# Reordering the settled slots of a cross-attention and FP4 feed-forward layer, with one ff2 bank for each row half

## The reference, cut to what matters

```python
# x (8, 512, 256); ctx (8, 64, 256); dff 1024; FP4 ffn width 704
y = layernorm0(x)                                    # 1
y = layernorm(y + attention(y, y, y, causal=True)) * g1 + beta1
y = layernorm(y + attention(y, ctx, ctx)) * g2 + beta2      # cross-attention
y = layernorm(y + relu(y @ w1 + b1) @ w2 + b2) * g3 + beta3 # ff1, ff2
x = x + y
xq = fp4(layernorm(x))                               # blocks of 16, scale max/6, round to a grid
h = silu(xq @ fp4(w_gate).T) * (xq @ fp4(w_up).T)
out = x + fp4(h) @ fp4(w_down).T
```

## Time and profile before

| what | us |
|---|---|
| median of 3 runs | 597.99 (596.93 to 598.6) |
| the profiled execution, its own time | 599.96 |
| its span, first to last instruction | 597.4 |
| TensorE busy | 561.2 (94%) |
| VectorE busy | 495.2 (83%) |
| ScalarE, GpSimd busy | 374.4 (63%), 383.1 (64%) |
| mean granted TensorE clock | 0.994 |

### The profile page before, as it was taken

One profiled execution on the slowest core, in us unless ns is written; L12 is line 12 of the kernel. 1 busy time (PEld: TensorE's weight loads), 2 busy tenths in 40 slices (PEclk: granted clock), 3 DMA queues, 4 the chain that ended last, 5 costly groups with the idle time before them and its releaser, 6 DMA issues.

```text
span 597.4 us, 12450 instructions
## 1 busy us (share of the span) xinstructions
PE 561.2 (94%) x4042; PEld 532.7 (89%) x4042; DVE 495.2 (83%) x1222; ACT 374.4 (63%) x778; POOL 383.1 (64%) x463
## 2 busy tenths in 40 slices
PE   4787889999999999999999999999999999999985
PEld 3676789999999999999999999999999999999885
DVE  4989888887988888887988888887978878887776
ACT  3766565766667575766667575766667574756231
POOL 3668657676757667676757667675767656666542
PEclk9999989999999999999999999999999999999989
DMA  7701010010201001010201001010101010000000
GB/s 229 242 2 37 0 46 1 1 55 1 63 1 55 2 21 42 0 53 0 61 0 53 0 26 35 0 53 0 61 2 35 2 37 1 19 2 19 0 10 26
DMA packets 18742, 19.30 MB, mean 32 GB/s; under 512 B 1536, under 2 KB 18192, under 8 KB 18704
## 3 DMA queue, kind: packets, MB, share of 16 engines
q1 hardware_dynamic: 18704, 18.82, 10.3%
HBM read 14.62 MB, written 4.19 MB: 32 GB/s over the span
## 4 chain that ended last, share of the span: by engine, by line
PE 75%; DVE 6%; POOL 4%; issue 4%; ACT 1%; DVEq 0%; POOLq 0%; ACTq 0%
PE R L1119 6%; PE R L1121 6%; PE R L1120 6%; PE O L1171 5%; PE TR L1024 5%; PE O L1239 4%; PE O L1241 4%; PE O L1240 4%; PE R L1189 4%; PE R L1191 4%; PE R L1190 4%; PE O L1217 3%; PE O L1219 3%; PE O L1218 3%; PE R L1024 3%
## 5 line engine op out<-in xcount | busy, mean ns | idle before, releaser
L462 POOL TENSOR_TENSOR rs<-mv,neg_half 128x1 f32<-128x1 f32 (+1 forms) x112 | 68.4, 620 | 29.6 <-DVE mv L1588 28.3
L1119 PE MATMUL R<-gu_hi,xqT_hi 128*128 128x352 f32 x240 | 80.8, 337 | 2.9 <-ACT hT L742 1.9
L1189 PE MATMUL R<-y2T_hi,w_hi 128*128 128x256 f32 x256 | 76.4, 298 | 4.5 <-ACT e_diag L776 1.7
L753 ACT ACTIVATE hqT_hi<-R 128x768 fp32r<-128x768 f32 x29 | 23.6, 813 | 86.7 <-PE R L1024 86.7
L1121 PE MATMUL R<-gu_hi,xqT_lo 128*128 128x352 f32 x240 | 77.9, 325 | 0.0
L1120 PE MATMUL R<-gu_lo,xqT_hi 128*128 128x352 f32 x240 | 77.7, 324 | 0.0
L1239 PE MATMUL O<-w_hi,hT_hi 128*128 128x256 f32 x256 | 74.5, 291 | 1.1 <-POOL hT_lo L497 1.1
L1191 PE MATMUL R<-y2T_hi,w_lo 128*128 128x256 f32 x256 | 72.1, 282 | 0.0
L1190 PE MATMUL R<-y2T_lo,w_hi 128*128 128x256 f32 x256 | 72.0, 281 | 0.0
L1241 PE MATMUL O<-w_hi,hT_lo 128*128 128x256 f32 x256 | 71.9, 281 | 0.0
L1240 PE MATMUL O<-w_lo,hT_hi 128*128 128x256 f32 x256 | 71.8, 280 | 0.0
(11 more groups left out here) (193 smaller groups left out, 1826.5 us busy)
## 6 DMA issues: line engine op xcount, KB each, us to landing
x_in<-in_x SPq DMA_DIRECT2D x16, 256.0 KB, 2.8
x_res<-in_x SPq DMA_DIRECT2D x16, 256.0 KB, 2.8
out<-x SPq DMA_DIRECT2D x32, 128.0 KB, 1.9
ctx_rows<-in_ctx SPq DMA_DIRECT2D x16, 64.0 KB, 2.5
hT<-in_L_xattn_w SPq DMA_DIRECT2D x1, 1024.0 KB, 8.3
hh<-in_L_xattn_w SPq DMA_DIRECT2D x1, 768.0 KB, 7.5
wd_raw<-in_L_ffn_w_down SPq DMA_DIRECT2D x1, 704.0 KB, 9.1
w_raw<-in_L_ffn_w_gate SPq DMA_DIRECT2D x1, 640.0 KB, 4.5
```

Of the source, the lines that this page charges most:

```text
L1119: mm(o, xh, gu_hi[:, c, m, cols], start=(c == 0), stop=False)
L1189: mm(o, w1_hi[:, c, cols], y2T_hi[:, c, :], start=(c == 0), stop=False)
```

## The change

The order of the calls in `slot` is rewritten on GpSimd, ScalarE, TensorE and VectorE, and ff2 gets a bank for each row half (O[0] for t = 0, O[1] for t = 1, except in the first ff2, of slot 2). The bank gives new waits: `values(0)` also waits for ff_sum(0) of the slot before, and ff2 of t = 0 for cross_sum (z2_set). ff2 is called in steps of two f for t = 0 and of four, two and two for t = 1. `early` names slot 3. The Silu `warm` moves behind `silu(b, h, 1, (0,))`.

```diff
+        def ff2_bank(b, h, t):
+            first = isinstance(b, int) and HALVES * b + h == F
+            return O[1 if first else t][:, 0:D]
...
@@ GpSimd slot
                 if f1:
                     gamma3(b, g, 0)
                     x1_sum(b, g, 0)
+                if f1 and early:
+                    w_unscaled(5)
                 if q1:
                     unscale_h(b, g, 1)
                 if f1:
                     power(4, b, g, F, (0,))
                     power(3, b, g, F, (1,))
...
+                if a:
+                    power(1, b, h, A, (0, 1))
+                if f1:
                     gamma3(b, g, 1)
                     x1_sum(b, g, 1)
+                    scale_x(b, g, 0)
+                    power(4, b, g, F, (1,))
+                if front:
+                    masks(b, h)
+                if f1:
                     unscale_x(b, g, 0)
+                    scale_x(b, g, 1)
+                    unscale_x(b, g, 1)
                 if f:
                     y_rows(b, h, False, 0)
+                    residual(b, h)
+                if a:
+                    y_rows(b, h, True, 0)
+                    y_rows(b, h, True, 1)
+                if f:
                     y_rows(b, h, False, 1)
+                if live(b, h + 1, 0):
+                    power(0, b, h + 1, 0, (0, 1))
                 if q:
                     scale_h(b, h, 0)
                 if f:
                     h_lower_last(b, h)
+                if front and h == 0:
+                    context_values(b)
+                if a:
+                    power(2, b, h, A, (0, 1))
                 if q:
                     unscale_h(b, h, 0)
...
@@ ScalarE slot, from norm(3, b, g, F, 1) on
+                if early:
+                    relu(b, h, (1,))
+                if a:
+                    norm(1, b, h, A, 0, 1, z1[:, 0, :], z1[:, 0, :])
+                    norm(1, b, h, A, 1, 1, z1[:, 1, :], z1[:, 1, :])
+                if f and (not early):
+                    relu(b, h, (0, 1))
                 if front:
                     exp_scores(b, h)
+                if f1:
+                    abs_x(b, g, 0)
+                if front:
                     exp_rest(b, h)
                 if f:
+                    relu_upper(b, h, (0,))
+                if a:
+                    affine_turned(b, h, A, n1_turned, y1T, g1_col, beta1_col, y1T_set)
+                if early:
+                    w_upper(act, 5)
+                if f:
+                    relu(b, h, (2,))
                 if f1:
                     abs_x(b, g, 1)
+                if q:
+                    xT_upper(b, h, 0)
+                if a:
+                    exp_cross(b, h)
                 if f:
+                    relu_upper(b, h, (1,))
+                    relu(b, h, (3,))
                 if q:
                     silu(b, h, 0, (0,))
+                    xT_upper(b, h, 1)
                 if f:
                     relu_upper(b, h, (2,))
+                if a:
+                    cp_upper(b, h)
                 if q:
                     silu(b, h, 0, (1,))
+                    silu(b, h, 1, (0,))
+                    warm(b, h, ACT.Silu, 0)
                 if f:
                     relu_upper(b, h, (3,))
                 if q:
                     silu(b, h, 1, (1,))
                     abs_h(b, h, 0)
...
@@ values, ff2
                     wait(pe, z2_set, b, h, F, T, T)
+                    wait(pe, z3_set, b, h, F + 1, T, 1)
...
-                    if fs[0] == 0:
-                        wait(pe, x2_set, b, h, Q + 1, T, T)
-                else:
-                    wait(pe, z3_set, b, h, F, T, 1)
-                o = O[1][:, 0:D]
+                first = isinstance(b, int) and HALVES * b + h == F
+                if fs[0] == 0:
+                    if t == 1 and first:
+                        wait(pe, z3_set, b, h, F, T, 1)
+                    if t == 0 and not first and live(b, h, A):
+                        wait(pe, z2_set, b, h, A, T, T)
+                    wait(pe, x2_set, b, h, Q + 1, T, t + 1)
+                o = ff2_bank(b, h, t)
...
@@ TensorE slot
+                if early:
+                    w_turn(4, FC, HEAD, 0)
                 if q1:
                     down(b, h - 1, 0)
...
                     scores_rest(b, h, range(T))
+                if a:
+                    turn_z1(b, h)
                 if q1:
                     down(b, h - 1, 1)
+                if early:
+                    w_turn(5, FC + FC // 2, 0, 0)
                 if f:
                     ff1(b, h, (4, 5))
+                if a:
+                    cross(b, h)
                 if q:
                     turn_xq(b, h, 0)
...
                     gate_up(b, h, 0, 0)
+                if a:
+                    turn_cross(b, h)
+                if q:
                     turn_xq(b, h, 1)
                     gate_up(b, h, 0, 1)
                     gate_up(b, h, 1, 0)
                 if a:
+                    cross_values(b, h)
                 if q:
                     gate_up(b, h, 1, 1)
                 if f:
                     ready_for_ff2(b, h)
+                    ff2(b, h, 0, (0, 1))
+                    ff2(b, h, 0, (2, 3))
+                    ff2(b, h, 0, (4, 5))
+                    ff2(b, h, 0, (6, 7))
+                    ff2(b, h, 1, range(0, 4))
                 if q:
                     turn_hq(b, h, 0)
+                if f:
+                    ff2(b, h, 1, (4, 5))
                 if front and h == 0:
                     turn_context(b)
                 if f:
+                    ff2(b, h, 1, (6, 7))
```

More of the change, by code:

```diff
@@ L516, in slot @@
                 f1, q1 = live(b, h, Q), live(b, h, Q + 1)
+                front = live(b, h, 0)
                 g = h - 1
+                early = isinstance(b, int) and HALVES * b + h == Q
                 if f1:
@@ L893, in slot @@
                     norm(2, b, h, A, 1, 1, z2[:, 1, :], z2[:, 1, :])
+                if q and a:
+                    hT_upper(b, h, 0)
+                    abs_h(b, h, 1)
+                if front and h == 0:
+                    context_turned(b)
             def abs_rows(b, h, t):
@@ L1761, in slot @@
                 g = h - 1
+                early = isinstance(b, int) and HALVES * b + h == Q
                 if a:
-                    self_reciprocal(b, h, 0)
-                    self_sum(b, h, 0)
+                    self_part(b, h, 0)
                 if q1:
                     h_lift(b, g, 1)
+                if early:
+                    w_lift(5)
+                if q1:
                     h_drop(b, g, 1)
@@ L1769, in slot @@
                     y2T_lower(b, h)
-                if isinstance(b, int) and HALVES * b + h == Q:
-                    w_lift(5)
+                if early:
                     w_drop(5)
                 if f1:
+                    x1_stats(b, g, 0)
+                    aggregate(4, b, g, F, 0)
                     z3_stats(b, g, 1)
-                    x1_stats(b, g, 0)
+                if a:
+                    self_part(b, h, 1)
+                if f1:
                     aggregate(3, b, g, F, 1)
-                    aggregate(4, b, g, F, 0)
-                if isinstance(b, int) and HALVES * b + h == Q:
+                if a:
+                    self_stats(b, h)
+                if early:
                     w_lower(4)
+                if f1:
+                    shift(3, b, g, F, (1,))
+                    x_norm(b, g, 0)
+                if q1:
+                    hT_lower(b, g, 1)
                 if a:
-                    self_reciprocal(b, h, 1)
-                    self_sum(b, h, 1)
+                    shift(1, b, h, A, (0, 1))
                 if f1:
-                    x_norm(b, g, 0)
                     x_max(b, g, 0)
@@ L1832, in slot @@
                     h_product(b, h, 0, 1)
+                if a:
+                    cp_lower(b, h)
+                if q:
                     h_max(b, h, 0)
+                if front:
+                    aggregate(0, b, h + 1, 0, 1)
+                if q:
                     h_scale(b, h, 0)
```

219 lines of the change are left out of this document (66 added, 153 removed).

## The result

The changed kernel takes 594.27 us (median of 7 runs, 593.18 to 595.52), the kernel before, run between them, 598.60 (7 runs, 596.93 to 600.75). The ratio is 0.9927, with a 95% interval from 0.9905 to 0.9948: faster by 0.7%, more than a measurement's 0.3%. I had forecast 591, 586 to 598. The profiled execution has a span of 592.4 us against 597.4.

The account below looks back on a forecast made before the run. TensorE was taken to bound the kernel, so a reorder gains only what it loses between groups. Settled slots -5.8, slot 3 -1.8, slot 16 -0.6, slot 17 +1.3 sum to -6.9 us: median 591 us, range 586 to 598.

Parts of the forecast that it names:

- Sign and range: Whole kernel: faster, at 591 us, with a range of 586 to 598; chance of faster by more than 1.8 us 0.72.
- Term 1: TensorE between groups, slots 4 to 15: fewer hand-overs and waits save 0.62 even, 0.84 odd, 1.46 us a pair.
- three hand-overs fewer: TensorE, settled slots: fp32 work handing over to f32r costs 0.09 each time, so the new order saves 0.27.
- the second bank: ff2 in settled slots: row half 1 no longer loses 0.16 us a slot to ff_sum(0) on the one bank.
- Term 2: Settled slots: new waits, chiefly turn_hq(0) behind ScalarE, VectorE and GpSimd, cost 0.5 us a pair; bounds 0 and 2.8.
- rival (B): ScalarE's Silu load on the live path makes silu later by a further 1.28 us: +16.3, 607 us; chance 0.14.
- Rival (A): VectorE is later than summed, 0.6 us a slot more, 7.2 us back: 598, no change; chance 0.14.
- Term 3: Slot 3: waits for exp_rest and Relu shrink, w_lift(5), scores and Silu load cost: -1.8 us, bounds +1 and -5.7.
- The scores' wait: Slot 3: scores must wait for w_lower(4), now behind self_stats, +1.4 us.
- w_lift(5): Slot 3: delays y2T_lower by 0.9 to 1.2, of which w_turn(4) covers 0.66: +0.5 us.
- I let the 1.2 GHz stretch stay: Slot 3: the low-clock stretch remains, since it followed waits of 1.55 and 1.94 and others take their place.
- Term 4: Slots 16 and 17: slot 16 saves 0.6 us; slot 17 loses 1.3 as turn_xq(0) gets its input late.

Follow-up runs that it names:

- experiment 3: The changed kernel with turn_context put back directly behind turn_hq(0): 594.94 us (one run), even slots 33.70, unchanged.
- experiment 9: The changed kernel with both row halves of ff2 in the one bank O[1], as before the change: 601.42 us (one run).
- experiment 4: The changed kernel with ff2 of row half 0 in two steps (five f, then three) in place of four: 598.68 us (one run).
- experiment 6: The changed kernel with GpSimd's residual on one column of each row (rest of that sum left out): 593.35 us (one run).
- experiment 10: The changed kernel with GpSimd's residual and y_rows of slots 6 to 13 on one column (rest left out): 593.45 us (one run).
- experiment 1: The changed kernel with Relu in place of Silu, so that no table is switched: 594.24 us (10 runs), ratio 0.992.
- experiment 5: The kernel before the change, unchanged, profiled once more: 597.07 us (one run), span 594.6.
- experiment 8: The changed kernel with turn_z1 behind down(1) in slot 16 alone: 594.74 us (5 runs), ratio 0.9906, slot 16 32.26 us.

## Why the prediction was right, and where it was not

**Sign and range** held: the new order takes waits from between TensorE's groups, VectorE's new queue gives part back, slot 17 pays. The range says little by itself, since it reached up to 598, the time before. The sum was -6.9 us against -5.0 in the profiles, and 1.6 of those 5.0 are the clock's. Without it the parts are -2.35, -2.85, 0 and +1.4, some -3.8, so the saving was little more than half of the sum.

**Term 1** was too large: 1.10 us a pair is what the slots would have saved if the new waits are simply taken off (33.64 - 33.15 and 33.31 - 32.70), not 1.46. The step that failed is "each place where fp32 work hands over to f32r costs 0.09", and three hand-overs fewer. The rows of turn_z2 between two groups of values and those around scores and turn_z1, first before, then after:

```profile
301.76 0.60 PE L1024 MATMUL TR<-ident,w_raw 128*128 128x128 f32 x4
302.20 1.03 PE L1171 MATMUL O<-y,e_full 128*128 128x257 f32 x4
...
310.47 1.03 PE L1140 MATMUL R<-y0T 128*128 128x256 f32 x4
311.14 0.47 PE L1217 MATMUL O<-wd_hi,hqT_hi 128*128 128x256 f32 x1
311.45 0.28 PE L1218 MATMUL O<-wd_lo,hqT_hi 128*128 128x256 f32 x1
...
322.55 0.60 PE L1024 MATMUL TR<-ident,z 128*128 128x128 f32 x4
322.90 0.41 PE L1119 MATMUL R<-gu_hi,xqT_hi 128*128 128x352 f32 x1
323.14 0.32 PE L1120 MATMUL R<-gu_lo,xqT_hi 128*128 128x352 f32 x1
```

```profile
305.65 1.03 PE L1148 MATMUL R<-y0T 128*128 128x256 f32 x4
306.52 0.60 PE L1032 MATMUL TR<-ident,z 128*128 128x128 f32 x4
306.88 0.36 PE L1226 MATMUL O<-wd_hi,hqT_hi 128*128 128x256 f32 x1
307.08 0.28 PE L1227 MATMUL O<-wd_lo,hqT_hi 128*128 128x256 f32 x1
```

Before, the first f32r matmul behind scores took 0.31 where 0.12 is usual, and the one behind turn_z1 0.24 where 0.16 is. This looks like a loss of 0.19 and 0.08 us, but none of it is lost. Where fp32 work follows, four turns take 0.44 to the next start (301.76 to 302.20) and the four wide matmuls of scores 0.87 (305.65 to 306.52). Where f32r work follows, the same groups show only 0.35 (322.55 to 322.90) and 0.67 (310.47 to 311.14). So the next group's first row starts 0.09 or 0.20 early, and its first step is longer by the same 0.08 or 0.19. From the start of the fp32 group to the second f32r matmul the sum is the same in both cases within 0.01: the long first step is the end of the fp32 work itself., which gives turn_z1 its whole 0.44, says it already. A hand-over costs nothing that these rows show, and putting two groups together saves nothing, as experiment 3 found for turn_context.

What remained of the term came from elsewhere. cross_values takes 0.47 to the next group instead of 0.61, 0.13 in either slot. ff2's matmuls, whose steps before held the wait ahead of cross_values (I had 0.20 and 0.33), that for ff_sum(0) and the turns between them, take 0.3 less in the even slot and 0.5 less in the odd one, the new waits taken off; how these divide I can't tell from the rows. I had put the second bank at 0.16 a slot, its price in the old order. In the new one it is worth 0.5 a slot, since ff_sum(0) stands behind h_drop(0) (experiment 9): without it slots 4 to 15 would be 3.6 us longer than before the change.

**Term 2** was right in its place and its chain and small in its size: 0.53 + 0.28 = 0.81 us of waits a pair, I had 0.5. It had no wait ahead of ff2: cross_sum was to end at 8.4 for a place wanted at 8.6, and ended at 8.79. The prediction summed VectorE's queue from durations of before, in which h_lower(2) did not meet y_rows; it does now, and takes 1.00 for 0.68. Experiments 4, 6 and 10 show it, and experiment 10 gives its price, the 0.2 us ahead of ff2 in an even slot. The wait ahead of turn_hq(0), 0.29 and 0.23 where I had 0.15, does not hang on it: it has the 0.14 behind cross_sum and the 0.13 between unscale_h(0) and turn_hq(0), for which the sum had nothing. The load of the Silu table, on which rival (B) rested, is hidden in the loop and costs 0.2 us in two unrolled slots (experiment 1), so (B) had neither its price nor its point. Rival (A), VectorE later than summed, came true by a quarter: 0.16 a slot beyond my sum and not 0.6. What I held against it, that fewer of VectorE's steps meet GpSimd, was wrong for the step that mattered.

**Term 3** was small in size, -1.8 for -2.35 (experiment 5). Its waits came out as the earlier trace rows suggested: exp_rest's 1.55 is gone, gate_up's 1.94 is 0.37, and scores wait for w_lower(4). TensorE's waits in slot 3 after the change:

```profile
PE R L1198 <- DVE y2T_lo L1732: 1.2, 1, 1.2
PE R L1145 <- DVE wd_lo L1565: 0.8, 1, 0.8
```

The scores' wait is 0.8 for my 1.4, and w_lift(5) added nothing to y2T_lower's 1.3, for my +0.5. "I let the 1.2 GHz stretch stay" was wrong for the execution profiled: there it lies in the head (from 46.4 us) and not in slot 3. Experiment 5 shows that the order before does not always have it in slot 3 either. None of the twelve profiles with the new order, the experiments' included, has one there; against one of two with the old order that leaves the cause open.

**Term 4.** Slot 17 was right in place and queue: 1.02 us at turn_xq(0) for unscale_x. That its sum came out too, +1.4 for +1.3, is luck. The slot's first three groups, up to turn_hq, take 1.2 us longer as well (4.72 for 3.48) and its last ones behind ff2 1.1 longer (5.75 for 4.67); from turn_xq(0) to the end of ff2 it is 1.9 less (16.39 for 18.30). None of these three stood in my sum. Slot 16 gave nothing for -0.6: turn_z1 waits 1.53 and not 0.9 (experiment 8).

**What the profile was to show:** a pair of 66.66 us and not 66.0; cross_values without a wait, yes; three fewer first-matmul delays, no; waits of 0.1 to 0.3 before turn_hq(0), yes; VectorE without idle, yes; slot 3 near 36, no, 33.73; slot 17, yes.

## What to carry to other kernels

Before pricing a regrouping of TensorE's work, ask whether the loss seen at a junction is one: compare two places where different work follows the same group, and sum from the start of the old group to the second matmul of the new. When steps move on VectorE, look again at which GpSimd instructions now start beside those with two SBUF inputs, since durations read before the move don't hold there. And a safeguard such as a second bank has the price of the order that it stands in, which may be several times its price in the old one.

## What was not expected of the hardware

- Two settled slots with the same program differ by 0.39 us because two instructions start within 0.01 us of each other: VectorE 1.29 and GpSimd 0.74, or 0.68 and 1.28. An execution with a small edit elsewhere can have the other length, as in experiment 3, and it looks then like an effect of the edit.
- The first f32r matmul behind fp32 work is recorded early, by 0.20 us behind the 128x256 scores and by 0.09 behind the turn of z, and its step to the next is longer by as much. It looks like a loss at the hand-over and is none.
- Stretches of 3.4 to 10.2 us at 1.2 GHz stand in other places from one execution to the next: the kernel before has one in slot 3 in one profile (37.64 us) and none there in the other (36.08); over all profiles heads are 61.3 to 64.4 us long. The kernel before alone ranged over 4 us in its 7 runs, while its settled slots agree within 0.1 us between two profiles.
